# Two attention layers with expert layers on one core: tile counts, an even share of expert pieces in every pair, and the order of VectorE's work in it

## The chip, the core and the metric

The kernel runs on one core of a Trainium2 chip. The core has a matrix engine (TensorE, PE in the profile; PEld is its loading of weights), VectorE (DVE), ScalarE (ACT), GpSimd (POOL) and a sync engine (SP) that starts most transfers. Each engine runs its own list of instructions in order, and they meet by semaphores. The metric is the device time of one execution in microseconds (us), lower is better.

## The reference

The input is eight sequences of 512 rows, 256 wide. There are two layers, and each adds an attention and a mixture of experts to its input, both fed by the layer-normed rows:

```python
xn = _layernorm(x)
x = x + _L0_attn_ref(xn, ...) + _L0_ffn_ref(xn, ...)
xn = _layernorm(x)
x = x + _L1_attn_ref(xn, ...) + _L1_ffn_ref(xn, ...)
```

`_L0_attn_ref` is a latent attention (16 heads of 16) with a norm over each head of the queries and keys and a causal softmax. `_L0_ffn_ref` sends each row to 4 of 8 experts:

```python
gate = jnp.minimum(gate, SWIGLU_LIMIT)
up = jnp.clip(up, -SWIGLU_LIMIT, SWIGLU_LIMIT)
act = (up + 1.0) * gate * jax.nn.sigmoid(SWIGLU_ALPHA * gate)
```

`_L1_attn_ref` is a causal attention with sparsemax in place of softmax. `_L1_ffn_ref` has an own grouped-query attention with rotation, then 2 of 8 experts per row, whose activation is `silu(g) * u`, and a clipped residual.

## The kernel before

Each of the three attentions works on a sequence in eight **pairs** (two heads each): 3 attentions by 8 sequences by 8 pairs are 192 pairs, numbered G from 0. The first 64 pairs are the latent attention ("mla"), the next 64 the grouped one ("gqa"), the last 64 the sparse one ("spm"). In a sequence, p = G mod 8 numbers the pairs. The expert rows are sorted by expert beforehand into **tiles** of 256 rows, with each expert's rows padded to whole tiles. 4096 rows with 4 choices are 64 full tiles. Tiles beyond those in use hold padding and are computed all the same.

**Two stages carry experts beside attention.** `SPANS` gives them: pairs 0 to 49 carry the 72 tiles of the first layer, pairs 138 to 177 the 40 tiles of the second. A tile s is four halves of work with the inner width cut in two (m = 0, 1). In `plan` they are a list of **pieces**, for each m: "gate" (12 matmuls, L771, into bank2), "up" (12 matmuls, L771, into bank3) and "down" of the tile before (12 matmuls, L791, into bank4). The list is cut into equal shares for the pairs, and each share into six slots q = 0..5 that stand between the steps of the pair's attention. For 72 tiles in 50 pairs that is 432 pieces, 8 or 9 in a pair, and the cut falls on another piece in each pair. For 40 tiles in 40 pairs it is 6 in each.

**PE in a pair with experts** does: turn the shifted queries (L745, `bank<-ident,qst`), turn the output of the pair before (`bank<-ident,oT`), slot 0, first half of the key scores (L817, L827), turn queries and keys of the next pair (`ident,qst` and `ident,kst`), slot 1, second half of the key scores, slot 2, query scores of the next pair (L824), slot 3, their second half, slot 4, outputs (L894), slot 5, and in p = 1 to 4 a projection for the next sequence (L846, two banks). After each "up" with m = 0 it also turns the rows of the next tile (`bank<-ident,xs`).

**Banks.** In these stages the turns, projections and outputs share two banks, bank0 and bank1, in strict alternation (class `Ring`). A bank is free again when the engine that reads it says so. The turned rows of a tile are read twice: ScalarE rounds them into `xh` (L1422) and VectorE then makes the remainder `xl` (`rest`, L1637), which frees the bank.

**The activation of a half tile** in the first layer goes over four engines: VectorE clips the gate (`clip_gate`, L1649, frees bank2), ScalarE takes its tanh (`gate`, L1402), VectorE clips the up half (`clip_up`, L1663, frees bank3), then `multiply`: L1672 joins the tanh and L1675 makes the product `t`. ScalarE rounds it (`high`, L1417), GpSimd makes its remainder (`low`, L1240), and "down" may use both. `multiply` and, behind it, `rest` or `pick_weight` (L1629, L1632) are put off: they are done before the next "gate" or at three fixed places of the pair (`finish`). In the second layer ScalarE applies silu straight from bank2 and VectorE has the one product L1682.

**Other work of VectorE in a pair**: `heads_out` of the pair before (L1917 to L1923), in p = 0 the statistics of the next sequence (`row_stats`) and, at the end, its `normalize` (L1736), in p = 2 to 5 `head_squares`, then `maxima` (L1831 or L1829) and `shift` for the next pair. `norm_heads` (L1780 to L1788) scales queries and keys of the next mla sequence: four heads at the end of p = 5, twelve at the end of p = 6. GpSimd's `stack` for two pairs later waits for it at p = 0 and p = 2.

After the first stage GpSimd gathers expert outputs into the accumulator by indirect transfers (four pairs from the second after the stage, and from pair 55), and after the second one 16 units of such adds are shared by the pairs left.

Of the kernel before, what the change touches and what calls it, by code (L numbers as in the profile page):

```python
# [24 lines left out]
F32 = mybir.dt.float32  # L25
# [16 lines left out]
NTOK = B * T  # L42
TS = 256
# [6 lines left out]
CHOICES = (4, 2)  # L50
# [4 lines left out]
TILES = (72, 40)  # L55
FIRST_TILE = (0, 72)
SPANS = ((0, 50), (138, 178))
# [89 lines left out]
def build(nc, dram, outs, ctx):  # L147
# [494 lines left out]
    def pipeline(kinds, its, mems, em=None, general=False):  # L642
# [14 lines left out]
        for layer, (a, b) in enumerate(SPANS if em else ()):  # L657
# [66 lines left out]
        with block as block:  # L724

            @block.tensor
            def _(pe):
# [25 lines left out]
                def up(s, m, side):  # L753
# [10 lines left out]
                    if g >= 1:  # L764
                        pe.wait_ge(used, g)
# [467 lines left out]
            def _(pool):  # L1233
# [14 lines left out]
                def stack(G):  # L1248
# [10 lines left out]
                    if p == 2 and kind == "mla":  # L1259
# [133 lines left out]
            def _(act):  # L1393
# [225 lines left out]
            def _(dve):  # L1619
                chain = Chain(dve, dve_step)  # L1620
                late = []
# [31 lines left out]
                def clip_up(g):  # L1653
# [3 lines left out]
                    bias = em["gu"][s % 2][:, 2 * GU:2 * GU + 8].bitcast(F32)  # L1657
                    dve.wait_ge(u_full, g + 1)
                    if g >= 2:
                        dve.wait_ge(al_ready, g - 1)  # L1660
                    for h in range(2):
                        j = FC + 2 * m + h
                        ins = dve.tensor_scalar(t[:, TS * h:TS * (h + 1)], up_bank[:, TS * h:TS * (h + 1)],  # L1663
                                                bias[:, j:j + 1], LIMIT + 1.0, ALU.add, ALU.min)
                    ins.then_inc(u_used, 1)

                def multiply(g):

                    t = em["t"][g % 2]
                    if layer_of(g // 2) == 0:  # L1670
                        dve.wait_ge(th_ready, g + 1)
                        chain(dve.scalar_tensor_tensor(em["gc"][:, :], em["th"][:, :], 1.0, em["gc"][:, :],  # L1672
                                                       ALU.add, ALU.mult))
                        dve.wait_ge(u_used, g + 1)
# [10 lines left out]
                def experts(G, q):  # L1685
                    for what, s, i in plan[G][q]:
                        if what == "gate":
                            finish()
                            if layer_of(s) == 0:
                                clip_gate(2 * s + i)  # L1690
                        if what == "up":
                            if layer_of(s) == 0:
# [642 lines left out]
```

## Time and profile before

| | |
|---|---|
| time, three runs | 3400.03, 3402.33, 3407.31 us (median 3402.33) |
| the profiled execution | 3404.42 us, of which 3402.4 us are the traced span |
| PE, DVE, ACT, POOL busy | 85%, 64%, 49%, 42% of the span |
| mean granted PE clock | 0.968 |
| first stage with experts | about 320 to 1515 us |
| second stage with experts | about 2480 to 3231 us |

All pairs of the profile can be found by their 16 output matmuls (L894) on PE. The number in square brackets behind an instruction is the time for which its engine sat idle before it, and what ended that.

### The profile page before, as it was taken

The page shows a single profiled execution, that of the slowest core. Times are in us where ns is not written, and L with a number is a line of the kernel's source. Part 1 is how long each engine was busy: PE and PEld are TensorE (multiplying, and loading weights), DVE is VectorE, ACT ScalarE, POOL GpSimd, SP SyncE. Part 2 cuts the span into 40 slices and gives each one's busy share as a digit, 9 for nine tenths or more (in the row PEclk, how much of TensorE's full clock was granted, in tenths as well). Part 3 has the DMA queues.
Part 4 walks back from the last instruction along what each step waited for, and adds up shares of the span by engine and source line. Part 5 has one row for each costly group of instructions (what it writes and reads, how often), then busy time and mean ns, then how long its engine had stood idle before and what let it go on. Part 6 is the DMA issues. An engine that isn't in the chain of part 4 may idle for free. (4 is left out here: it accounts for less than half of the span.)

```text
span 3402.4 us, 61952 instructions
## 1 busy us (share of the span) xinstructions
PE 2902.5 (85%) x21678; PEld 2326.9 (68%) x21678; DVE 2166.4 (64%) x6249; ACT 1659.2 (49%) x3466; POOL 1433.8 (42%) x2037
## 2 busy tenths in 40 slices
PE   4414989989998999987998888898899999999996
PEld 3312778777878778775666666666578888888864
DVE  4544677777767677755777777766745455454565
ACT  1201445444454545444666665665545555555553
POOL 3753333424242433328555666532322222222277
PEclk9997999999999999988999999999899999999998
DMA  8852556556665666632233333322155555555455
GB/s 270 300 214 107 221 224 244 221 223 230 231 238 222 223 223 222 243 127 39 50 89 92 100 100 100 91 86 72 48 220 215 203 215 210 207 212 199 153 101 120
DMA packets 193735, 587.54 MB, mean 173 GB/s; under 512 B 22984, under 2 KB 145808, under 8 KB 158608
## 3 DMA queue, kind: packets, MB, share of 16 engines
q1 hardware_dynamic: 156560, 532.40, 42.5%
q0 software_dynamic: 36864, 51.14, 7.4%
q8 instruction: 177, 2.90, 0.3%
q14 instruction: 134, 1.10, 0.1%
HBM read 456.99 MB, written 126.48 MB: 171 GB/s over the span
## 5 line engine op out<-in xcount | busy, mean ns | idle before, releaser
L1240 POOL TENSOR_TENSOR al<-t,ah 128x512 fp32r<-128x512 f32 x224 | 293.2, 1309 | 1097.8 <-ACT ah L1417 1097.8
L771 PE MATMUL bank<-xh,gu 128*128 128x256 f32 x3584 | 658.8, 288 | 8.1 <-DVE t L1682 2.4
L817 PE MATMUL bank<-masks_bf,ident_bf 128*128 128x128 bf16 (+1 forms) x2304 | 579.1, 251 | 90.8 <-ACT ksT L1499 40.7
L1831 DVE TENSOR_REDUCE st<-bank 128x1 f32<-128x512 f32 (+3 forms) x1024 | 423.9, 482 | 208.1 <-PE bank L824 206.9
L1512 ACT ACTIVATE pt<-bank 128x512 f32<-128x512 f32 (+1 forms) x1152 | 513.4, 538 | 83.3 <-PE bank L827 81.0
L771 PEld LDWEIGHTS bank<-xh,gu 128*128 128x128 f32 x3584 | 523.2, 193 | 25.9 <-issue 17.2
L817 PEld LDWEIGHTS bank<-masks_bf,ident_bf 128*128 128x128 bf16 x2304 | 224.9, 98 | 358.2 <-issue 78.3
L827 PE MATMUL bank<-qaT,ksT 128*128 128x512 f32 (+3 forms) x1536 | 436.0, 391 | 0.0
L824 PE MATMUL bank<-ksT,qsT 128*128 128x512 f32 (+3 forms) x1536 | 434.7, 380 | 0.0
L1520 ACT ACTIVATE oT<-bank 128x512 f32<-128x512 f32 x192 | 114.4, 596 | 514.6 <-PE bank L894 514.6
L771 PE MATMUL bank<-xl,gu 128*128 128x256 f32 x1792 | 362.0, 284 | 0.0
L824 PEld LDWEIGHTS bank<-ksT,qsT 128*128 128x128 f32 x1536 | 282.9, 205 | 3.4 <-issue 1.3
L827 PEld LDWEIGHTS bank<-qaT,ksT 128*128 128x128 f32 x1536 | 280.7, 203 | 0.3
L771 PEld LDWEIGHTS bank<-xl,gu 128*128 128x128 f32 x1792 | 280.5, 193 | 0.0
L745 PE MATMUL bank<-ident,qst 128*128 128x128 f32 x1536 | 237.5, 278 | 49.1 <-POOL kst L1282 36.3
L791 PE MATMUL bank<-dn,ah 128*128 128x256 f32 x1792 | 263.5, 290 | 14.7 <-POOL al L1240 9.3
L1417 ACT ACTIVATE ah<-t 128x512 fp32r<-128x512 f32 x224 | 141.4, 631 | 252.6 <-DVE t L1675 213.8
L894 PE MATMUL bank<-pt,V 128*17 128x512 f32 (+3 forms) x3072 | 256.5, 453 | 0.7 <-ACT pt L1512 0.7
L1829 DVE MAX8 top<-bank 128x8 f32<-128x512 f32 (+3 forms) x512 | 213.7, 484 | 58.0 <-PE bank L824 55.5
L791 PEld LDWEIGHTS bank<-dn,ah 128*128 128x128 f32 x1792 | 231.8, 193 | 20.7 <-issue 20.7
L745 PEld LDWEIGHTS bank<-ident,qst 128*128 128x128 f32 x1536 | 178.3, 142 | 86.1 <-POOL kst L1282 39.4
L1319 POOL DMA_INDIRECT acc<-ys_scratch,slots x128 | 204.4, 1597 | 44.9 <-issue 34.2
(249 smaller groups left out, 5282.6 us busy)
## 6 DMA issues: line engine op xcount, KB each, us to landing
gu<-wu_scratch SPq DMA_DIRECT2D x112, 2056.0 KB, 7.8
dn<-wd_scratch SPq DMA_DIRECT2D x112, 1024.0 KB, 9.4
xs<-xs_scratch SPq DMA_DIRECT2D x112, 264.0 KB, 8.9
ys_scratch<-yb SPq DMA_DIRECT2D x112, 256.0 KB, 9.6
raw<-in_gu SPq DMA_DIRECT2D x16, 1024.0 KB, 10.6
wu_scratch<-hi SPq DMA_DIRECT2D x16, 1024.0 KB, 5.4
wu_scratch<-lo SPq DMA_DIRECT2D x16, 1024.0 KB, 4.0
xs_scratch<-empty SPq DMA_DIRECT2D x32, 264.0 KB, 3.2
```

What stands on the lines that cost most here:

```text
L745: mm = pe.transpose(bank[:, P * n:P * (n + 1)], b, ident[:, :])
L771: mm = pe.matmul(bank[:, TS * h:TS * (h + 1)], gu[:, col:col + P], x[s % 2][:, TS * k:TS * (k + 1)], start=(n == 0), stop=(n == len(terms) ...
L791: mm = pe.matmul(down_bank[:, D * half:D * (half + 1)], a[s % 2][:, j // 2, tok:tok + P], dn[:, part + D * j:part + D * (j + 1)], start=(n ...
L817: pe.matmul(bank[:, diag:diag + P * len(unit)], ident_bf[:, :], masks_bf[:, 0 if which == "q" else 1, 0:len(unit), :].rearrange("p n k -> ...
L824: mm = pe.matmul(bank[:, first:first + width], mem["qsT"][:, P * blk:P * (blk + 1)], ks[:, 0:width], start=False, stop=end, skip_group_che ...
L827: mm = pe.matmul(bank[:, first:first + width], ks[:, P * blk:P * (blk + 1)], mem["qaT"][:, T - width:T], start=False, stop=end, skip_group ...
L894: mm = pe.matmul(bank[q0:q0 + HD + 1, P * kb:T], V[n % 2][:, kb, vh, :], pt[:, j, PT_AT[kb]:PT_AT[kb] + T - P * kb], start=(kb < 2), stop= ...
L1240: pool.tensor_tensor(em["al"][s % 2][:, m, :], em["t"][g % 2][:, :], em["ah"][s % 2][:, m, :].bitcast(F32), ALU.subtract).then_inc(al_read ...
L1319: pool.indirect_dma_start(acc[:, NT * b + t, :], None, ys_dram, at, compute_op=ALU.add).then_inc(gathered[i], 16)
L1512: act.activation(to, frm, ACT.Relu if kind == "spm" else ACT.Exp).then_inc(s_act, 1)
L1829: ins = dve.max(top[:, 0, r, :], bank[:, first:first + width])
L1831: ins = dve.reduce_max(st[:, 0, r:r + 1], bank[:, first:first + width], AX.X)
```

## The change

The tile counts become 64 + 7 = 71 and 32 + 7 = 39, which is the most that the padding can need. The shares are fixed by `PIECES`: nine pieces in each pair of the first stage and six in each of the second, so the stages are pairs 0 to 47 (the last with three pieces) and 138 to 176. VectorE's `clip_up`, `multiply` and `finish` are joined in `activate`, which stands wholly at the "up" piece, in the order tanh product, clip of the up half, product. ScalarE's tanh and silu move from the "up" piece to the "gate" piece. `norm_heads` is cut 8 and 8, stands behind slot 0 of p = 6 and p = 7, and GpSimd waits for its second part at p = 4. `normalize` in p = 0 stands ahead of slot 2.

```diff
+TILES = tuple(NTOK * k // TS + E - 1 for k in CHOICES)
+FIRST_TILE = (0, TILES[0])
+PIECES = (9, 6)
+SPANS = tuple((a, a - -6 * t // n) for a, t, n in zip((0, 138), TILES, PIECES))
...
-                own = work[len(work) * (G - a) // (b - a):len(work) * (G - a + 1) // (b - a)]
+                own = work[PIECES[layer] * (G - a):PIECES[layer] * (G - a + 1)]
...
                     if g >= 1:
-                        pe.wait_ge(used, g)
+                        pe.wait_ge(used, 3 * g if used is u_used else g)
...
-                    if p == 2 and kind == "mla":
+                    if p == NP // 2 and kind == "mla":
...
                 def experts(G, q):
                     for what, s, i in plan[G][q]:
-                        if what == "up":
+                        if what == "gate":
                             highs()
                             gate(2 * s + i)
-                            late.append(2 * s + i)
+                        elif what == "up":
                             if i == 0 and not last_tile(s):
                                 take_x(s + 1)
-                        elif what == "down":
+                            late.append(2 * s + i)
+                        else:
...
+                def activate(g):
...
+                    if layer_of(s) == 0:
+                        bias = em["gu"][s % 2][:, 2 * GU:2 * GU + 8].bitcast(F32)
                         dve.wait_ge(th_ready, g + 1)
+                        dve.scalar_tensor_tensor(em["gc"][:, :], em["th"][:, :], 1.0, em["gc"][:, :],
+                                                 ALU.add, ALU.mult).then_inc(u_used, 1)
+                        dve.wait_ge(u_full, g + 1)
+                        if g >= 2:
+                            dve.wait_ge(al_ready, g - 1)
+                        for h in range(2):
+                            j = FC + 2 * m + h
+                            dve.tensor_scalar(t[:, TS * h:TS * (h + 1)], up_bank[:, TS * h:TS * (h + 1)],
+                                              bias[:, j:j + 1], LIMIT + 1.0, ALU.add, ALU.min).then_inc(u_used, 1)
+                        dve.wait_ge(u_used, 3 * (g + 1))
                         dve.scalar_tensor_tensor(t[:, :], t[:, :], 1.0 - LIMIT, em["gc"][:, :],
                                                  ALU.max, ALU.mult).then_inc(a_ready, 1)
...
                         if what == "up":
-                            if layer_of(s) == 0:
-                                clip_up(2 * s + i)
-                            late.append((s, i))
...
+                            activate(2 * s + i)
+                            if not last_tile(s):
+                                if i == 0:
+                                    rest(s + 1)
+                                else:
+                                    pick_weight(s + 1)
...
                     experts(G, 0)
+                    if is_at(n + 1, "mla") and p >= 6:
+                        norm_heads(n + 1, slice(H // 2 * (p - 6), H // 2 * (p - 5)))
                     experts(G, 1)
-                    finish()
...
+                    if n + 1 < nb and p == 0:
+                        normalize(n + 1)
                     experts(G, 2)
-                    finish()
```

On PE, the end of pair 2 of the first stage stood like this before. L771 into bank3 is an "up" piece with m = 0, L791 a "down" piece, L846 the projection:

```order
L771 MATMUL bank3<-xh0_1728,gu0_1732 128x256 x2
L745 MATMUL bank0<-ident,xs1_1727 128x128 x4
L791 MATMUL bank4<-dn1_1735,ah1_1715 128x256 x8
L791 MATMUL bank4<-dn1_1735,al1_1717 128x256 x4
L846 MATMUL bank1<-w_mla_1698,xT 128x512
L846 MATMUL bank0<-w_mla_1698,xT 128x512
L745 MATMUL bank1<-ident,qst1_1676 128x128 x4
L745 MATMUL bank0<-ident,oT_1685 128x128 x4
```

Now every pair from 1 to 46 holds down, gate and up, down, gate and up, down, gate and up in its slots. In pairs with odd p the last "up" has m = 0. This is the end of pair 1, line numbers one higher:

```order
L772 MATMUL bank3<-xh1_1729,gu1_1733 128x256 x2
L746 MATMUL bank0<-ident,xs0_1726 128x128 x4
L847 MATMUL bank1<-w_mla_1698,xT 128x512
L847 MATMUL bank0<-w_mla_1698,xT 128x512
L746 MATMUL bank1<-ident,qst0_1675 128x128 x4
L746 MATMUL bank0<-ident,oT_1685 128x128 x4
```

The turned tile rows (`xs`) and the second projection share bank0. The down piece that stood between them is gone from there.

On VectorE, the end of pair 14 (p = 6) and the start of pair 15 stood like this before; `both` is the first step of `heads_out`:

```order
L1649 TENSOR_SCALAR gc_1718<-bank2,gu1_1733 128x256 x2
L1663 TENSOR_SCALAR t1_1721<-bank3,gu1_1733 128x256 x2
L1672 SCALAR_TENSOR_TENSOR gc_1718<-th_1719,gc_1718 128x512
L1675 SCALAR_TENSOR_TENSOR t1_1721<-t1_1721,gc_1718 128x512
L1629 TENSOR_TENSOR wtmp_1725<-xs0_1726,gu0_1732 128x16
L1632 TENSOR_REDUCE wsel1_1723<-wtmp_1725 128x2
L1780 TENSOR_TENSOR qk_mla0_1692<-qk_mla0_1692,qkn_1699 128x4x192 x2
L1785 TENSOR_TENSOR qk_mla0_1692<-qk_mla0_1692,qkw_1700 128x4x192 x2
L1788 TENSOR_TENSOR qk_mla0_1692<-qk_mla0_1692 128x4x192
L1917 COPY both_1691<-bank1 128x136
```

Now the end of an odd pair of the first stage, behind its maxima, is two whole activations and the start of the next pair:

```order
L1650 TENSOR_SCALAR gc_1718<-bank2,gu0_1732 128x256 x2
L1661 SCALAR_TENSOR_TENSOR gc_1718<-th_1719,gc_1718 128x512
L1668 TENSOR_SCALAR t1_1721<-bank3,gu0_1732 128x256 x2
L1671 SCALAR_TENSOR_TENSOR t1_1721<-t1_1721,gc_1718 128x512
L1630 TENSOR_TENSOR wtmp_1725<-xs1_1727,gu1_1733 128x16
L1633 TENSOR_REDUCE wsel0_1722<-wtmp_1725 128x2
L1650 TENSOR_SCALAR gc_1718<-bank2,gu1_1733 128x256 x2
L1661 SCALAR_TENSOR_TENSOR gc_1718<-th_1719,gc_1718 128x512
L1668 TENSOR_SCALAR t0_1720<-bank3,gu1_1733 128x256 x2
L1671 SCALAR_TENSOR_TENSOR t0_1720<-t0_1720,gc_1718 128x512
L1638 TENSOR_TENSOR xl0_1730<-bank0,xh0_1728 128x512
L1903 COPY both_1691<-bank0 128x136
```

The instruction that joins the tanh (now L1661) has moved ahead of the clip of the up half (now L1668), and the head norm is no longer between the last activation and `both`.

## Rows read from the trace of the kernel before

**Rows 1.** The page, busy time of each engine (us, share of span, instructions)

```profile
PE 2902.5 (85%) x21678; PEld 2326.9 (68%) x21678; DVE 2166.4 (64%) x6249; ACT 1659.2 (49%) x3466; POOL 1433.8 (42%) x2037
```

**Rows 2.** Busy time by stretch; columns: stretch, us, PE, PEld, DVE, ACT, POOL, PEclk, DMA, GB/s

```profile
722.60:912.60 190.00, 176.35 (x1409) 153.07 (x1409) 139.56 (x334) 92.37 (x190) 70.03 (x85) 0.99 0.61 229
872.80:876.20 3.40, 2.97 (x14) 2.97 (x15) 0.83 (x4) 1.18 (x2) 1.69 (x6) 0.50 0.88 308
...
2493.50:3230.00 736.50, 710.41 (x5597) 601.44 (x5598) 367.12 (x1205) 383.29 (x781) 184.02 (x357) 1.00 0.55 202
```

**Rows 3.** Waits of PE from 320 to 1511: us in total, times, longest

```profile
PE bank L745 <- DVE xl L1637: 26.8, 17, 2.1
PE bank L745 <- DVE both L1918: 24.3, 9, 5.0
```

**Rows 4.** VectorE at the end of pair 23: start, us, instruction [idle before]

```profile
887.40 0.87 DVE L1649 TENSOR_SCALAR gc<-bank,gu 128x256 f32<-128x256 f32 x2
888.18 0.87 DVE L1663 TENSOR_SCALAR t<-bank,gu 128x256 f32<-128x256 f32 x2
888.97 0.69 DVE L1672 SCALAR_TENSOR_TENSOR gc<-th,gc 128x512 f32<-128x512 f32 x1
889.69 0.69 DVE L1675 SCALAR_TENSOR_TENSOR t<-t,gc 128x512 f32<-128x512 f32 x1
890.30 0.68 DVE L1637 TENSOR_TENSOR xl<-bank,xh 128x512 fp32r<-128x512 f32 x1
...
894.41 0.26 DVE L1918 TENSOR_TENSOR both<-both,bank 128x102 f32<-128x102 f32 x1
```

**Rows 5.** ScalarE in the same stretch

```profile
888.30 0.63 ACT L1402 ACTIVATE th<-gc 128x512 f32<-128x512 f32 x1 [7.02 <-DVE gc L1649]
...
890.42 0.63 ACT L1417 ACTIVATE ah<-t 128x512 fp32r<-128x512 f32 x1 [1.00 <-DVE t L1675]
...
891.80 0.63 ACT L1402 ACTIVATE th<-gc 128x512 f32<-128x512 f32 x1
```

**Rows 6.** PE from the outputs of pair 23 to those of pair 24

```profile
887.02 1.27 PE L894 MATMUL bank<-pt,V 128*17 128x512 f32 x16
...
892.04 0.63 PE L745 MATMUL bank<-ident,oT 128*128 128x128 f32 x4
...
895.38 0.60 PE L745 MATMUL bank<-ident,kst 128*128 128x128 f32 x4
...
908.29 1.27 PE L894 MATMUL bank<-pt,V 128*17 128x512 f32 x16
```

**Rows 7.** PE behind the last "up" of pair 47

```profile
1462.44 0.60 PE L745 MATMUL bank<-ident,qst 128*128 128x128 f32 x4
1465.15 0.63 PE L745 MATMUL bank<-ident,oT 128*128 128x128 f32 x4 [2.12 <-DVE xl L1637]
```

**Rows 8.** PE, projection at the end of pair 27

```profile
984.26 1.02 PE L846 MATMUL bank<-w_mla,xT 128*128 128x512 f32 x2
985.45 1.12 PE L846 MATMUL bank<-w_mla,xT 128*128 128x512 f32 x2 [0.16 <-DVE xl L1637]
```

**Rows 9.** PE behind pair 32 (two rows), and at the end of the first stage

```profile
1110.33 1.16 PE L745 MATMUL bank<-ident,xb 128*128 128x128 f32 x8 [2.85 <-DVE xb L1736]
1111.24 1.65 PE L791 MATMUL bank<-dn,ah 128*128 128x256 f32 x8
...
1512.29 2.04 PE L791 MATMUL bank<-dn,ah 128*128 128x256 f32 x8 [4.20 <-POOL al L1240]
```

**Rows 10.** VectorE, the twelve-head part of the norm behind pair 14

```profile
678.25 2.89 DVE L1780 TENSOR_TENSOR qk_mla<-qk_mla,qkn 128x768 f32<-128x768 f32 x2
...
683.03 0.96 DVE L1788 TENSOR_TENSOR qk_mla<-qk_mla 128x768 f32<-128x768 f32 x1
```

**Rows 11.** PE, pair 160 of the second stage, and pair 185 of the tail

```profile
2912.13 1.21 PE L745 MATMUL bank<-ident,xb 128*128 128x128 f32 x8 [0.57 <-DVE xb L1736]
...
3319.84 0.86 PE L745 MATMUL bank<-ident,qst 128*128 128x128 f32 x4 [2.39 <-POOL kst L1282]
```

More of the change, by code:

```diff
@@ L42 @@
 NTOK = B * T
+CHOICES = (4, 2)
 TS = 256
@@ L49 @@
 GB = 2 * GU + 16
-CHOICES = (4, 2)
 TABLE = 80
-TILES = (72, 40)
-FIRST_TILE = (0, 72)
-SPANS = ((0, 50), (138, 178))
+TILES = tuple(NTOK * k // TS + E - 1 for k in CHOICES)
+FIRST_TILE = (0, TILES[0])
+PIECES = (9, 6)
+SPANS = tuple((a, a - -6 * t // n) for a, t, n in zip((0, 138), TILES, PIECES))
 FIRST_GATHERS = 55
@@ L1620, in _ @@
                 chain = Chain(dve, dve_step)
-                late = []
                 def pick_weight(s):
@@ L1686, in experts @@
                     for what, s, i in plan[G][q]:
-                        if what == "gate":
-                            finish()
-                            if layer_of(s) == 0:
-                                clip_gate(2 * s + i)
+                        if what == "gate" and layer_of(s) == 0:
+                            clip_gate(2 * s + i)
                         if what == "up":
-                            if layer_of(s) == 0:
-                                clip_up(2 * s + i)
-                            late.append((s, i))
-                def finish():
-                    while late:
-                        s, i = late.pop(0)
-                        multiply(2 * s + i)
-                        if not last_tile(s):
-                            if i == 0:
-                                rest(s + 1)
-                            else:
-                                pick_weight(s + 1)
+                            activate(2 * s + i)
[4 more added lines that the diff above has]
+                                    pick_weight(s + 1)
                 def row_stats(n):
@@ L2041, in pair_with_experts @@
                         experts(G, q)
-                    finish()
                     if is_at(n - 1, "spm") and p == 1:
                         residual(n - 1)
-                    if n + 1 < nb and p == 0:
-                        normalize(n + 1)
-                    if is_at(n + 1, "mla"):
-                        if p == 5:
-                            norm_heads(n + 1, slice(0, 4))
-                        if p == 6:
-                            norm_heads(n + 1, slice(4, H))
                 def pair_alone(G):
@@ L2087, in pair_alone @@
                         normalize_again(n + 1)
-                    if is_at(n + 1, "mla"):
-                        if p == 5:
-                            norm_heads(n + 1, slice(0, 4))
-                        if p == 6:
-                            norm_heads(n + 1, slice(4, H))
+                    if is_at(n + 1, "mla") and p >= 6:
+                        norm_heads(n + 1, slice(H // 2 * (p - 6), H // 2 * (p - 5)))
                     if is_at(n, "gqa") and 1 <= p <= 3:
@@ L2107, in _ @@
                     chain(dve.tensor_scalar(mems["mla"]["qkw"][:, 0, :], mems["mla"]["qkw"][:, 0, :], 0.25, None, ALU.mult))
-                    norm_heads(0, slice(0, 4))
+                    norm_heads(0, slice(0, H // 2))
                 maxima(0, range(NU))
@@ L2111, in _ @@
                 if kinds[0] == "mla":
-                    norm_heads(0, slice(4, H))
+                    norm_heads(0, slice(H // 2, H))
                 for G in range(steps):
```

17 lines of the change are left out of this document (removed).

## The prediction

> **What bounds the kernel now.** The page first: PE is busy for 85% of the span and the next engine, VectorE, for 64% [rows 1]. So I read what PE does and waits for, stage by stage. In eight pairs of the first expert stage PE works 176.4 of 190.0 us at clock 0.99; in the second stage 710 of 736.5 us at 1.00 [rows 2]. The second is nearly full. The first has 13.6 us of idle PE in eight pairs, 1.7 per pair, and that is where the change can win or lose. The waits of PE there name VectorE at both ends: 26.8 us in 17 waits for `xl`, 24.3 us in 9 for `both` [rows 3]. Both free one of the two shared banks. VectorE is not the busiest engine but the one that is late at the end of a pair, because its maxima end late and two activations queue behind them [rows 4].
>
> **A pair that already stands in the new order.** From the outputs of pair 23 to those of pair 24 the pieces lie exactly as they will lie everywhere: gate and up, down, gate and up, down, gate and up, down. This takes 21.27 us (908.29 less 887.02 [rows 6]) with 9 pieces and no PE wait over 0.5 us. It is my yardstick. A pair of mean share takes 190.0 / 8 = 23.75 us for 8.64 pieces.
>
> **The change, part by part.**
>
> *Two tiles less.* A tile is six pieces of 12 matmuls, 1.44 us each by the spacing in the trace at full clock (one piece of 8 + 4 matmuls: 1.5 us at L791), and 0.44 us for turning its rows: 9.1 us. PE is the bound in both stages, so two tiles give -18.2 us. If one hid behind other waits it would be -9.
>
> *The end of the first stage.* Before, the last two downs wait 4.20 us for the last remainder from GpSimd [rows 9], then 0.66 us more, and 10 us pass at half clock, which costs some 5. Now two idle slots stand between the last up and the last downs. Two pairs also leave the stage and their 1.7 us of idle each. 4.9 + 5 + 3.4 is -13 us (bounds: 0, and -18 if all that PE idles in the last pairs goes).
>
> *Even shares, with VectorE's order as it was.* Eight yardstick pairs are 170.2 us. Four carry a projection, 2.2 us each (from 984.26 to 986.5 by both rows [rows 8]), 8.8; one carries the turned rows of the next sequence, 1.2 [rows 9]. In the four pairs behind an odd p the last up has m = 0, its turned rows hold a bank, and the second turn or projection behind it waits for `xl`: 2.12 us in pair 48 [rows 7], four times 8.4. Sum 188.6 us for 72 pieces. The stage before needs 190.0 for 69.1 pieces; 2.9 more at 1.44 make 194.1. So -5.5 us per eight pairs, and for 47 intervals -32 us. In this the wait for head norms (up to 5.0 us, once in eight pairs [rows 3]) is gone: the twelve-head part keeps VectorE from 678.25 to 683.99 ahead of `both` [rows 10]. Now two parts of eight heads, some 3.5 us each by the same rate, stand behind `both`, while PE does a down, three score units and two turns.
>
> *VectorE's new order in an activation.* This is the step that decides. Before, the clip of the up half (888.18, next start 888.97: 0.79 us) runs while ScalarE makes the tanh (888.30 to 888.93) [rows 4, 5]. The tanh costs VectorE nothing. Now L1672's step comes ahead of the clip. VectorE is idle from 888.2 to 888.97, then joins, clips and multiplies: `t` comes 0.79 us later. Two activations follow each other behind the maxima, both with VectorE late, so 1.6 us. ScalarE's `ah`, `yb` and `oT` now stand between the first product and the second tanh, by the spacing 890.42 to 891.80 [rows 5] another 0.3. `xl`, which frees the bank in the odd pairs, is 1.9 us later: 4 x 1.9 = 7.6 per eight pairs. In the even ones PE waits 0.75 us for bank3, since the up half is now clipped at 890.4 and not at 888.97 where PE wants it at 889.8 (1.44 behind the gate piece that starts at 888.3, when bank2 is free), and in two of them `both` (894.41 before) is late too, for a turn that PE wants at 895.4 [rows 4, 6]: 0.75 twice, 1.1 and 1.75, 4.3. Sum 11.9 us per eight pairs, +70 us for 47 intervals. Bounds: 0, if VectorE has slack there that I don't see, and +75 (two times 0.79 in each of 47 pairs).
>
> *The clock.* After a wait of 2.85 us the clock falls to half: a down takes from 1111.24 to 1113.5 us, 2.3 us, where it takes 1.5 at full clock [rows 9]; after 2.59 us it stands at 0.50 for 3.4 us [rows 2]. All nine such waits of PE of 2.59 us or more in this stage are followed by such a stretch, of some thirteen of about 2 us only two. The odd waits grow from 2.1 to about 3.2 us (the bank 1.9 later, PE itself 0.75 later), with a projection 2.8. A stretch loses half of 3.4 us, 1.7. Five of eight pairs could have one; I take three, +5.1 per eight pairs, +30 us (bounds 0 and +50). The Trainium skill ("TensorE: Matmul & The Clock Gate", HAM oscillation) describes the same for a loop in which each round waits: the penalty is paid in every round, as half of the throttled time. By that rule all five pairs pay and the sum is 20 us higher; the trace agrees on the half, and on two-microsecond waits it mostly doesn't pay.
>
> *Small parts.* `normalize` earlier in p = 0 ends a wait of 0.57 us in five pairs of the second stage [rows 11], -2.5. Tanh and silu move ahead on ScalarE: 0, its silu was already waiting for nothing but bank2, and the 1.07 us waits for `xl` in that stage stay, since `xh` waits for the turned rows. The 16 units of adds are now shared by 15 pairs and only the last has two: the 2.39 us wait [rows 11] goes, -2.4. The first norm at the start has 8 heads and not 4, +1.4. In pair 54, without experts, the norm now stands at VectorE's end and GpSimd's `stack` behind it, and the first thing PE does in pair 55 is to turn its result: about 3.5 for the norm, 2.3 for the stack, +6 (0 to +9). Bringing GpSimd's gathers two pairs forward: 0, they collide with the same kind of pair.
>
> **The sum** against the profiled execution, 3404.4: -18.2 - 13 - 32 + 70 + 30 - 2.5 - 2.4 + 1.4 + 6 = +39, so 3443.7. The median of the three runs is 2.1 us lower, and I predict 3441 us.
>
> **Rivals.**
>
> *A. VectorE's order costs nothing.* The even shares win and the new wait is absorbed, since VectorE is only 73% busy in this stage (139.6 of 190 [rows 2]). For it: the idle share. Against it: at the end of a pair VectorE works without a pause from 887.40 to 894.67 [rows 4], and a bank hangs on each end. Then 3404.4 - 18.2 - 13 - 32 + 2.5, about 3343 us. This is the other side, faster; it decides if the bank waits behind odd pairs stay near 2.1 us. From the sum it takes a cost of order plus clock under 55 us for any gain at all.
>
> *B. Order costs, clock doesn't.* The waits grow, but the clock stays up, as it did in most waits near 2 us. Then 3443.7 - 30 - 2.1, about 3411 us, and down to 3398 if the order also costs less than reckoned.
>
> *C. Every late bank is paid in full.* With a strict turn of two banks every delay of `xl` goes to PE at its full length, and all five waits in eight pairs take their stretch at half clock: 3441 plus two more stretches in eight pairs (1.7 x 2 x 5.9 = 20), 3461 us. For it: all nine waits of 2.59 us or more had one. Against it: with a projection the wait is 2.8 us only by my working. The Trainium skill ("Perfetto Trace Analysis", Optimization Strategy) reads the same gap repeating on the engine that should be full as a sign of too few buffers in PSUM; the 17 waits for `xl` [rows 3] agree.
>
> *D. It doesn't do what it says.* Tiles 72 and 40 might be in use. The bound of 71 follows from the padding, and a tile too few would change the result, not the time; I leave this no chance of its own.
>
> **How the numbers follow.** My forecast with its own range of 3420 to 3455 us: 0.45. C: 0.13. B: 0.17. A and what lies between it and no change: 0.25. Three runs of this kernel spread by 0.2%, so no change is within 6.8 us of 3402.3. Faster than 3395.5: A, 0.25, and a little of B, 0.02. Same: most of the lower half of B, 0.09. Slower: 0.64. The range of 8 in 10 leaves out the bottom of A and the top of C: 3348 to 3470 us. The likeliest case alone, slower, is 3410 to 3465.
>
> **What would show it.** Right: in pairs 1 to 46 the `oT` turn or the second projection behind odd p waits about 3 us for `xl`; PE waits some 0.7 us at bank3 ahead of the last up of a pair; VectorE shows an idle 0.7 us ahead of the tanh join, ended by ScalarE; eight pairs of the first stage take about 205 us, the clock there falls from 0.98 to about 0.95. Wrong on the order: eight pairs take 190 or less and the `xl` waits stay at 2. Wrong on the shares: waits in pairs with even p that the yardstick doesn't have. The second stage should keep its 151 us for eight pairs (736.5 / 39 x 8 [rows 2]) less 0.5, and the tail end 9 us after its tile. If GpSimd's `stack` shows up ahead of PE's turns at p = 7 within the stage, the head norms in two equal parts are what I mispriced.

## The result, and the profile after

The changed kernel takes 3424.86 us (median of 5 runs, 3419.56 to 3426.56), the kernel before 3400.03 us (5 runs of the same chip, 3388.92 to 3407.31). The ratio is 1.0066, with a 95% interval of 1.0046 to 1.0086: slower by 0.7%. The profiled executions are 3426.6 us (span 3424.9) and 3404.4 us (span 3402.4), so 22 us are to be explained; the forecast was +39.

First the busy line of the page after, against [rows 1]: two tiles less are 152 matmuls less, yet PE is busy only 2 us less.

```profile
PE 2900.2 (85%) x21526; PEld 2315.0 (68%) x21526; DVE 2171.0 (63%) x6229; ACT 1649.7 (48%) x3452; POOL 1435.1 (42%) x2033
```

Busy time by stretch (us, PE, PEld, DVE, ACT, POOL, PEclk, DMA, GB/s) from the outputs of pair 14 to those of pair 22, and from those of pair 0 to those of pair 47. In the kernel before the same eight pairs took 188.8 us. The 190.00 us of [rows 2] are another stretch (it starts 1.9 us behind the outputs of pair 16), but the mean of eight pairs over that stage is 190.0 too.

```profile
702.50:907.10 204.60, 184.45 (x1421) 158.62 (x1423) 142.81 (x337) 92.66 (x190) 72.01 (x85) 0.97 0.59 220
343.40:1534.00 1190.60, 1073.77 (x8253) 920.85 (x8252) 832.29 (x1951) 543.35 (x1115) 423.86 (x498) 0.97 0.59 217
```

What PE waits for in the first stage (343 to 1534 us; total, times, longest). The waits for `xl` are longer than in [rows 3], and a new group stands third: the bank of the up half, which L1668 reads.

```profile
PE bank L746 <- DVE xl L1638: 30.0, 11, 2.7
PE bank L847 <- DVE xl L1638: 26.1, 12, 2.2
PE bank L772 <- DVE t L1668: 22.2, 47, 0.5
PE bank L746 <- DVE both L1904: 11.6, 7, 1.8
PE bank L818 <- ACT pt L1514: 9.0, 6, 1.7
PE bank L746 <- ACT oT L1522: 4.9, 23, 0.3
```

Where it comes from is seen at the end of a pair. VectorE at the end of pair 23 (start, us, instruction, idle before), against [rows 4]:

```profile
930.94 0.87 DVE L1650 TENSOR_SCALAR gc<-bank,gu 128x256 f32<-128x256 f32 x2
932.51 0.69 DVE L1661 SCALAR_TENSOR_TENSOR gc<-th,gc 128x512 f32<-128x512 f32 x1 [0.70 <-ACT th L1403]
933.12 0.87 DVE L1668 TENSOR_SCALAR t<-bank,gu 128x256 f32<-128x256 f32 x2
934.02 0.69 DVE L1671 SCALAR_TENSOR_TENSOR t<-t,gc 128x512 f32<-128x512 f32 x1
...
936.78 0.69 DVE L1661 SCALAR_TENSOR_TENSOR gc<-th,gc 128x512 f32<-128x512 f32 x1 [0.99 <-ACT th L1403]
937.38 0.87 DVE L1668 TENSOR_SCALAR t<-bank,gu 128x256 f32<-128x256 f32 x2
938.29 0.69 DVE L1671 SCALAR_TENSOR_TENSOR t<-t,gc 128x512 f32<-128x512 f32 x1
938.90 0.68 DVE L1638 TENSOR_TENSOR xl<-bank,xh 128x512 fp32r<-128x512 f32 x1
```

And PE in the same place: it waits for the clip of the up half, then for `xl`.

```profile
934.04 0.51 PE L772 MATMUL bank<-xh,gu 128*128 128x256 f32 x2 [0.43 <-DVE t L1668]
936.37 0.63 PE L746 MATMUL bank<-ident,qst 128*128 128x128 f32 x4 [0.19 <-ACT oT L1522]
939.73 0.63 PE L746 MATMUL bank<-ident,oT 128*128 128x128 f32 x4 [2.73 <-DVE xl L1638]
```

That is VectorE's idle time ahead of the join, ended by ScalarE. It stands there in nearly every activation; its sum from 368 us to the end of the stage, where the kernel before has less than 1 us of it:

```profile
DVE gc L1661 <- ACT th L1403: 102.4, 137, 1.1
```

Along the program, by the start of a pair's outputs on PE (L895, before L894), the changed kernel is 43.2 us behind at pair 56 (1659.4 against 1616.2), 43.4 at pair 137, 28.2 at pair 178 and 22.5 at the end of the span. So the first stage and the pairs behind it lose 43 us, and the second stage with the tail wins 21.

### The profile page after: what moved, and what is told of

It is laid out like the page before. It is cut to its first block and busy times, and to the rows that moved or that the text cites. A ratio compares the mean times of both kernels' runs of the same rounds, so it can differ in the third digit from the quotient of the medians.

```text
span 3424.9 us, 61408 instructions
## 1 busy us (share of the span) xinstructions
PE 2900.2 (85%) x21526; PEld 2315.0 (68%) x21526; DVE 2171.0 (63%) x6229; ACT 1649.7 (48%) x3452; POOL 1435.1 (42%) x2033
## 5 line engine op out<-in xcount | busy, mean ns | idle before, releaser
L1241 POOL TENSOR_TENSOR al<-t,ah 128x512 fp32r<-128x512 f32 x220 | 286.3, 1301 | 1131.0 <-ACT ah L1418 1131.0
L772 PE MATMUL bank<-xh,gu 128*128 128x256 f32 x3520 | 636.8, 287 | 31.5 <-DVE t L1668 22.2
L772 PEld LDWEIGHTS bank<-xh,gu 128*128 128x128 f32 x3520 | 502.7, 190 | 62.7 <-DVE t L1668 31.6
L772 PE MATMUL bank<-xl,gu 128*128 128x256 f32 x1760 | 351.8, 281 | 0.0
L772 PEld LDWEIGHTS bank<-xl,gu 128*128 128x128 f32 x1760 | 271.4, 190 | 0.0
L1403 ACT ACTIVATE th<-gc 128x512 f32<-128x512 f32 x142 | 89.6, 631 | 370.7 <-DVE gc L1650 370.7
L895 PE MATMUL bank<-pt,V 128*17 128x512 f32 (+3 forms) x3072 | 256.3, 453 | 0.7 <-ACT pt L1514 0.7
L1418 ACT ACTIVATE ah<-t 128x512 fp32r<-128x512 f32 x220 | 138.6, 630 | 205.5 <-DVE t L1671 144.5
```

The costliest lines, as they stand in the source:

```text
L772: mm = pe.matmul(bank[:, TS * h:TS * (h + 1)], gu[:, col:col + P], x[s % 2][:, TS * k:TS * (k + 1)], start=(n == 0), stop=(n == len(terms) ...
L895: mm = pe.matmul(bank[q0:q0 + HD + 1, P * kb:T], V[n % 2][:, kb, vh, :], pt[:, j, PT_AT[kb]:PT_AT[kb] + T - P * kb], start=(kb < 2), stop= ...
L1241: pool.tensor_tensor(em["al"][s % 2][:, m, :], em["t"][g % 2][:, :], em["ah"][s % 2][:, m, :].bitcast(F32), ALU.subtract).then_inc(al_read ...
L1418: act.activation(em["ah"][s % 2][:, m, :], em["t"][g % 2][:, :], ACT.Copy).then_inc(ah_ready, 1)
```

## The experiments

Each differs from its base by the edit shown alone. "Stage" is the time from the outputs of pair 0 to those of pair 47 (before: to pair 49, 1163.9 us), "passage" from there to those of pair 57 (before: 118.3 us; changed: 1190.6 and 134.0). The kernel before was run again beside experiments 1 to 4, 5 to 8 and 9 to 12, with medians of 3403.9, 3399.3 and 3403.6 us. So kernels of different groups are compared by their ratios to it, and not by their medians.

**1. The clip first again** (base: the changed kernel; the counts of `u_used` that PE and VectorE wait for follow the edit).

```diff
 def activate(g):
+    # u_full, al_ready; clip both halves -> u_used
     dve.wait_ge(th_ready, g + 1)
     # join: gc <- (th + 1) * gc
-    # u_full, al_ready; clip both halves -> u_used
     # product: t -> a_ready
```

> The changed kernel with one thing put back: in an activation of the first expert layer VectorE clips the up half first and joins the tanh after it. Tiles, shares, norms and tail stay as changed. My theory (the order costs, the even shares win): `xl` comes 1.9 us earlier, the waits of PE for it behind odd pairs fall from 2.7 to about 2.1 us and the one ahead of the last up of a pair (0.5 us) goes; the 47 intervals of the stage fall from 1190.6 to about 1110 to 1125 us and the kernel takes 3345 to 3360 us. Rival 1 (the order costs nothing, the shares themselves are dear): within 5 us of the changed kernel, 3420 to 3430. Rival 2 (half and half): 3380 to 3395, with `xl` waits still above 2.4 us.

Measured: 3347.49 us, ratio to the kernel before 0.983 [0.9816, 0.9843]; stage 1110.3 us. PE's waits and the stage's busy time:

```profile
PE bank L746 <- DVE xl L1638: 21.4, 11, 2.0
PE bank L847 <- DVE xl L1638: 16.6, 12, 1.4
PE bank L746 <- ACT V L1475: 7.4, 24, 0.4
```

```profile
345.10:1455.40 1110.30, 1040.47 (x8257) 901.92 (x8259) 829.32 (x1951) 540.77 (x1115) 423.83 (x498) 0.99 0.63 233
```

One order of two VectorE steps is worth 77 us by the medians and 80 by the ratios. The group at L772 is gone, the waits for `xl` are 0.8 us shorter each. The stage's difference of 80.3 us is 47.0 us of idle PE (116.8 against 69.8) and 33.3 us of busy PE for the same matmuls. Part of the busy time is the clock (71.7 us at half clock against 27.3). Another part is found in the gate and up matmuls alone, of which none ran at half clock in either kernel (the stage again, PE and PEld of L772, first the changed kernel, then this one):

```profile
343.40:1534.00 1190.60, 437.20 (x3336) 406.53 (x3336) 0.97 0.59 217
345.10:1455.40 1110.30, 424.88 (x3336) 403.64 (x3336) 0.99 0.63 233
```

The same 3336 matmuls keep PE busy for 12.3 us more. The 47 waits at bank3 are the difference: a matmul that starts behind a pause adds 0.38 us of busy time here, and one in the stream 0.12.

**2. The join first, in the kernel before.**

```diff
 # multiply(g), at the next gate piece or at the pair's end
     join: gc <- (th + 1) * gc
+    clip_up(g)
     product: t
 # experts(): "up"
-    clip_up(2 * s + i)
```

> The kernel before with one thing changed: VectorE joins the tanh first and clips the up half behind it, in every activation of the first expert layer. Tiles, shares and all else as before. Theory: the order costs by itself, with the old uneven shares as well; 0.8 us per activation, where a bank hangs on it, so +40 to +70 us, 3440 to 3470. Rival 1 (the order is harmless until the shares are even): within 7 us of the kernel before. Rival 2 (the old shares leave slack in most pairs): +10 to +30 us.

Measured: 3453.34 us, ratio 1.0147 [1.0132, 1.0161], so +50 us. The order costs by itself, also with the old shares; of PE's waits in its stage (`both`, 21.7 us in 9, is near [rows 3]):

```profile
PE bank L745 <- DVE xl L1637: 34.3, 21, 2.9
PE bank L771 <- DVE t L1663: 13.7, 20, 0.8
PE bank L745 <- ACT V L1473: 11.7, 24, 1.6
```

**3. Two tiles less, in the kernel before.**

```diff
-TILES = (72, 40)
-FIRST_TILE = (0, 72)
+TILES = (71, 39)
+FIRST_TILE = (0, 71)
```

> The kernel before with 71 and 39 tiles, all else as it was (the pieces are still spread over 50 and 40 pairs). Theory: PE bounds both stages, 9.1 us per tile, -18 us, 3382. Rival 1: one of the two hides behind waits of the first stage, -9 us, 3391. Rival 2: a tile less only lengthens the waits for the shared banks, within 5 us of the kernel before.

Measured: 3402.11 us, ratio 0.9994 [0.9984, 1.0005]. The second rival: no gain that can be measured. The profile shows 10.7 us won up to the outputs of pair 56 and given back in the second stage, which takes 770.9 us from pair 138 to 178 and took 760.6 with a tile more. 234 pieces in 40 pairs are 5.85 a pair; the pieces wander through the slots, and new waits come up (here 2482 to 3253 us):

```profile
PE bank L745 <- DVE xb L1736: 5.7, 5, 2.1
PE bank L745 <- ACT oT L1520: 5.5, 6, 1.6
PE bank L854 <- DVE xl L1637: 5.2, 4, 1.5
```

**4. Even shares alone, in the kernel before** (the stage ends after 48 pairs).

```diff
+PIECES = (9, 6)
-SPANS = ((0, 50), (138, 178))
+SPANS = tuple((a, a - -6 * t // n) for a, t, n in zip((0, 138), TILES, PIECES))
-own = work[len(work) * (G - a) // (b - a):len(work) * (G - a + 1) // (b - a)]
+own = work[PIECES[layer] * (G - a):PIECES[layer] * (G - a + 1)]
```

> The kernel before with nine and six pieces in each pair, so that the first stage ends after 48 pairs and not 50; 72 and 40 tiles, VectorE's order, the head norms and the tail's adds as before (but GpSimd's gathers move two pairs forward with the end of the stage). Theory: even shares give 45 us in the stage and at its end, and the pairs without experts behind it take some 12 us of that back, as in the changed kernel's trace (109.4 against 125.4 us to the outputs of pair 56): 3360 to 3372 us. Rival 1: the even shares win nothing, since every pair with odd p now stalls: 3395 to 3405. Rival 2: they lose: over 3410.

Measured: 3426.26 us, ratio 1.0066 [1.0052, 1.008]: slower, and my theory for this kernel fell (rival 2). Its stage takes 1163.7 us, 53.4 more than the first experiment's: 31.5 us of idle PE, and 78.5 us at half clock against 27.3. Two waits hold most of the idle time, for the head norms ahead of `both` and for `normalize`:

```profile
PE bank L746 <- DVE both L1919: 29.2, 6, 4.9
PE bank L746 <- DVE xl L1638: 21.4, 11, 1.9
PE bank L746 <- DVE xb L1737: 17.1, 6, 2.9
```

So what I had booked as the gain of even shares belongs to the shares together with two moves of VectorE's other work. Experiments 7 and 8 take these apart.

**5. Head norms a pair earlier behind the stage** (base: experiment 1).

```diff
 # pair_alone
-if is_at(n + 1, "mla") and p >= 6:
-    norm_heads(n + 1, slice(H // 2 * (p - 6), H // 2 * (p - 5)))
+if is_at(n + 1, "mla") and 5 <= p <= 6:
+    norm_heads(n + 1, slice(H // 2 * (p - 5), H // 2 * (p - 4)))
```

> The first experiment's kernel (clip first; 3347.5 us), with the two halves of the head norm at the ends of pairs 53 and 54 instead of 54 and 55, in pairs without experts alone. Theory: in pair 54 GpSimd's `stack` waits 11.1 us for the norm there, and PE then 6.8 us for `kst`; that PE wait falls to 2 or 3 us, and the kernel takes 3341 to 3344 us. Rival 1: GpSimd is late on its own account (four powers of some 5.5 us, two stacks and the gathers in these pairs), the wait is merely renamed, within 2 us of 3347.5. Rival 2: VectorE does the norm ahead of the maxima that PE's next scores wait for in pair 53, and loses elsewhere: 3348 to 3352.

Measured: 3339.94 us, ratio 0.9825 [0.9811, 0.9839]; the ratios don't tell it from experiment 1. The passage takes 130.5 us and not 134.6: 4.1 us by the profile. The stage ahead of it, in which nothing differs, was 4.0 us shorter than in experiment 1, so half of the difference of the profiled executions (8.5 us) is not the edit's.

**6. Gathers in pairs 51 to 54 again** (base: experiment 1).

```diff
-if em and ends_at[0] < G <= ends_at[0] + CHOICES[0]:
+if em and ends_at[0] + 2 < G <= ends_at[0] + 2 + CHOICES[0]:
     for i in range(2):
-        gather(0, G - ends_at[0] - 1, i)
+        gather(0, G - ends_at[0] - 3, i)
```

> The first experiment's kernel (3347.5 us), with the gathers of the first rows in pairs 51 to 54, where the kernel before has them, and no longer in 49 to 52. Theory: a gather's four issues cost GpSimd some 8 us in a pair that already has a power and a stack; the waits of PE for `kst` in pairs 50 to 52 (2.7, 3.9 and 6.0 us) shrink by 3 to 6 us in all, of which the later pairs, with the norm, give back some: 3340 to 3345. Rival: pairs 53 and 54 then carry both, the loss only moves, 3347 to 3353.

Measured: 3339.90 us, ratio 0.9824 [0.981, 0.9837], again not told from experiment 1 by the ratios; passage 128.5 us, 6.1 less. The step that I had priced at nothing is seen on GpSimd in the changed kernel, ahead of the pair whose `kst` comes 5.89 us late: a power, four gathers, and only then the stack.

```profile
1593.18 5.45 POOL L1307 TENSOR_TENSOR qkn<-qkn,minus_half 128x32 f32<-128x32 f32 x1
1598.82 1.62 POOL L1320 DMA_INDIRECT acc<-ys_scratch,slots  x1 [0.19 <-issue]
...
1604.97 1.54 POOL L1320 DMA_INDIRECT acc<-ys_scratch,slots  x1 [0.81 <-issue]
1605.94 0.88 POOL L1273 CAST qst<-qk_mla 128x128 fp32r<-128x128 f32 x1
...
1608.34 0.29 POOL L1283 COPY kst<-kst 128x128 f32<-128x128 f32 x1
...
1624.99 0.29 POOL L1273 CAST qst<-qk_mla 128x128 fp32r<-128x128 f32 x1 [10.95 <-DVE qk_mla L1774]
```

The last row is the wait for the head norm that the prediction named, in pair 54. PE's part, on the turns of the stacks of these pairs:

```profile
1593.27 0.85 PE L746 MATMUL bank<-ident,qst 128*128 128x128 f32 x4 [4.58 <-POOL kst L1283]
1608.68 1.11 PE L746 MATMUL bank<-ident,qst 128*128 128x128 f32 x4 [5.89 <-POOL kst L1283]
1627.16 1.12 PE L746 MATMUL bank<-ident,qst 128*128 128x128 f32 x4 [6.81 <-POOL kst L1283]
```

**7. Head norms as before** (base: experiment 1).

```diff
 # pair_with_experts, pair_alone, at their ends
-norm_heads in halves at p = 6, 7
+if p == 5: norm_heads(n + 1, slice(0, 4))
+if p == 6: norm_heads(n + 1, slice(4, H))
 # GpSimd's second wait for them: p == NP // 2 -> p == 2
```

> The first experiment's kernel (3347.5 us), with the head norms as in the kernel before: four heads at the end of p = 5, twelve at the end of p = 6. Theory: the wait of PE for `both` in the stage goes from 6 back to about 29 us, as in the kernel with even shares alone, and takes some half-clock stretches with it: 3375 to 3390 us. Rival 1: with VectorE's activations in one go the long part finds room, 3350 to 3360. Rival 2: at the stage's end it wins back what the pairs 53 to 55 lose, the whole 3365 to 3375.

Measured: 3366.76 us, ratio 0.9904 [0.9888, 0.9919], to experiment 1 +19 us by the profiled executions and +25 by the ratios: the second rival's size. The stage loses 27.5 us (1137.8), `both` is back, and the passage wins 6.6 (128.0). The row is from 368 us on; the whole stage has 36.1 us in 12 waits.

```profile
PE bank L746 <- DVE both L1905: 29.6, 10, 4.9
```

**8. `normalize` as before** (base: experiment 1).

```diff
 # pair_with_experts
-    if n + 1 < nb and p == 0:      # ahead of the third slot
-        normalize(n + 1)
 ...
+    if n + 1 < nb and p == 0:      # at the end
+        normalize(n + 1)
```

> The first experiment's kernel (3347.5 us), with `normalize` back at the end of pairs with p = 0. Theory: PE's wait for `xb` comes back, 2.9 us in each of five or six such pairs of the first stage (14 to 17 us in the kernel with even shares alone) and with some of them a stretch at half clock, 1.7 us; in the second stage 0.5 us in five pairs: 3363 to 3375 us. Rival: the turn of the rows moves behind other PE work that is there anyway, 3348 to 3355.

Measured: 3351.77 us, ratio 0.986 [0.9845, 0.9876], +10 us to experiment 1 by the ratios and by the profiled executions; stage 1115.8 us, +5.5. The wait of the theory is there (the row is from 368 us on; in the whole stage six waits, 17.1 us), but the price is nearer the rival's: those for `both` at the same turn (6.2 us) go, so that idle PE grows by 8.4 us.

```profile
PE bank L746 <- DVE xb L1723: 14.2, 5, 2.8
```

**9. Both moves of 5 and 6** (base: experiment 1; the two edits above together).

> The first experiment's kernel (clip first) with both moves at the end of the first stage: the halves of the head norm in pairs 53 and 54, the gathers in pairs 51 to 54. Theory: the two relieve different engines, and what each gave from the outputs of pair 47 to those of pair 57 (134.6 us, 130.5 with the norm moved, 128.5 with the gathers moved) adds up: about 124.5 us, 3330 to 3336 us in all. Rival: both relieve the same pile-up on GpSimd, 128 us, 3338 to 3342.

Measured: 3340.54 us, ratio 0.9812 [0.9799, 0.9825]; passage 122.8 us, 11.8 less than in experiment 1, so in the profile the two add up, and the passage of experiment 11, which has the same code there, takes 122.7. The times don't show it: the median lies in the rival's range (3338 to 3342), and the ratios don't tell 5, 6 and 9 apart.

**10. `xl` ahead of the product** (base: experiment 9).

```diff
 # activate, first layer: clip, join,
+    if between is not None:      # m = 0: the next tile
+        rest(between)            # xl
     dve.wait_ge(u_used, g + 1)
     # product: t -> a_ready
```

> The kernel of the ninth experiment with one more step: in the first expert layer VectorE makes `xl` of the next tile ahead of the product of the activation and not behind it. Theory: PE's waits for `xl` behind odd pairs (23 of them, 2.0 and 1.4 us) fall by 0.7 us each, 16 us in all, and a few stretches at half clock with them: 3312 to 3322. Rival: `t`, then `ah` and `al` come 0.7 us later and the downs or the next gate wait instead, within 4 us of the ninth. Rival 2: `xh` isn't there yet when VectorE asks for it and all of the activation waits: slower than the ninth by over 5 us.

Measured: 3325.94 us (3319.96 to 3327.17), ratio 0.9769 [0.9756, 0.9782], the fastest of all: 2.3% under the kernel before, 2.9% under the changed one. It missed the expected range all the same (3312 to 3322). The waits for `xl` fell by 14 us of the 16 reckoned; `oT` took part of it (9.6 us in 14 waits). The profiled execution is 15.5 us shorter than that of experiment 9: 7.9 us in the stage, 2.3 in the passage and 5.7 in pairs 57 to 137, where the edit changes nothing. So about half of the difference is placed at the edit. In the stage PE is busy 1032.1 of 1098.2 us at clock 1.00:

```profile
PE bank L746 <- DVE xl L1638: 14.8, 11, 1.4
PE bank L746 <- ACT oT L1522: 9.6, 14, 0.9
PE bank L847 <- DVE xl L1638: 9.4, 12, 0.8
```

```profile
343.60:1441.80 1098.20, 1032.08 (x8257) 890.61 (x8259) 845.05 (x1950) 540.02 (x1115) 422.73 (x498) 1.00 0.63 235
```

**11. The tail's adds in 14 pairs** (base: experiment 9).

```diff
-tail_pairs = range(ends_at[1], steps)
+tail_pairs = range(ends_at[1] + 1, steps)
```

> The kernel of the ninth experiment with the tail's 16 units of adds shared by the last 14 pairs and not by 15, as in the kernel before (two of them carry two). It prices the tail's part of the change. Theory of the prediction: +2.4 us. What the two traces say (28.2 us behind at the outputs of pair 179, 20.7 at the end): +7 us, with a stretch or two at half clock behind the wait for `kst`. Rival: nothing, since the last adds end the kernel in either case: within 2 us.

Measured: 3343.70 us, ratio 0.9823 [0.981, 0.9836]. From the outputs of pair 179 to the end it takes 140.0 us and the ninth kernel 134.1: 5.9 us. By the medians alone (+3.2, intervals overlap) it would be open, but all five profiled kernels with 14 pairs take 138.6 to 140.0 us there, and all nine with 15 take 132.6 to 134.1. PE shows a wait for `kst`, as in [rows 11], and one for the maxima behind it:

```profile
3264.35 0.66 PE L746 MATMUL bank<-ident,qst 128*128 128x128 f32 x4 [2.08 <-POOL kst L1283]
...
3279.43 0.28 PE L818 MATMUL bank<-masks_bf,ident_bf 128*128 128x256 bf16 x1 [1.74 <-DVE top L1816]
```

**12. The changed kernel with `xl` ahead of the product** (the edit of 10 in the changed kernel's order: join, clip, `xl`, product).

> The changed kernel as it is (tanh joined first, norms and gathers as changed), with `xl` of the next tile made ahead of the product. It asks how much of the order's cost hangs on the late `xl` and on the clock behind it. Theory: the 23 waits for `xl` (2.7 and 2.2 us) become 2.0 and 1.5, which is 16 us, and most of the 13 additional stretches at half clock go, up to 22 us: 3387 to 3409; the waits of PE at bank3 (47 of 0.5 us) stay. Rival 1: the clock's stretches don't depend on the length of these waits and stay at some 21: 3405 to 3412. Rival 2: PE then waits for `t` or `al`: within 7 us of 3424.9.

Measured: 3408.37 us (12 runs), ratio 1.0014 [1.0005, 1.0023], 16 us under the changed kernel, between theory and first rival. The waits at bank3 stayed, those for `xl` fell, and the clock rose from 0.97 to 0.99. The stage's 20.3 us are 13.7 us of busy PE and only 6.6 of idle (`oT` and `V` give back 10 us of the 17 that `xl` wins):

```profile
343.60:1513.90 1170.30, 1060.06 (x8257) 906.42 (x8260) 840.54 (x1951) 542.15 (x1115) 420.02 (x498) 0.99 0.60 221
```

```profile
PE bank L772 <- DVE t L1668: 22.2, 47, 0.5
PE bank L746 <- DVE xl L1638: 22.0, 11, 2.0
PE bank L847 <- DVE xl L1638: 17.3, 12, 1.5
```

## Why the prediction came out as it did

The direction and the mechanism were right and the size was 16 us too large. That it came so near is in part luck, since the smaller terms missed both ways (the gathers cost 6 us where I had 0, the tail won 5.9 where I had 2.4). Eight pairs took 204.6 us, where the sign said about 205, and the clock there was 0.97, not 0.95. Two readings of the prediction were loose: of the waits near 2 us in the stage before there are ten and not thirteen (two of them with a stretch at half clock), and 190 us is the mean of eight pairs, not a stretch from outputs to outputs. Step by step:

*Even shares with VectorE's order as it was*: forecast 188.6 us for eight pairs, 1108 for 47 intervals. Five profiled kernels have just this stage (experiments 1, 5, 6, 9, 11): 1110.3, 1106.3, 1106.4, 1106.1 and 1112.6. Right, but the gain hangs on the moves beside them: even shares alone lose (experiment 4). Of the 53 us between that stage and this one the norms in halves hold 27.5 (experiment 7) and the earlier `normalize` 5.5 (experiment 8). The rest, some 20, is the clock. Idle PE adds up (24.7 and 8.4 us against 31.5), but the stage of experiment 4 has 78.5 us at half clock, experiment 1 has 27.3, experiment 7 44.4 and experiment 8 23.9. That is 37.5 us more than the two moves bring one by one, and half of it is 19 us. Of its 12 stretches 11 last 6.8 us and not 3.4. Why they do, and what the activation in one go has to do with it, is not shown.

*VectorE's order, +70, and the clock, +30*: together 100, measured 80 in the stage and 77 in the medians (experiment 1). This is the term that was mis-sized. Between the two profiles the waits for `xl` grow by 18 us, those at bank3 by 22, `both` by 5, `pt` and `oT` by 7, less 4 for `V`; idle PE by 47 us in all. I had 45 for the late `xl` (PE's own delay with it) and 25 for the even pairs. `xl` comes 1.6 us later (7.96 against 6.38 us behind the start of the first `clip_gate`), where I had 1.9. PE arrives 0.8 us later by itself, for bank3 and `oT`, and the waits grow by 0.8 us, where I had 1.1. The bank3 wait is 0.5 and not 0.75 us, in every pair. But the restart behind it, which I had at nothing, keeps PE busy for 12.3 us more in 47 pairs (experiment 1), 0.26 us each. So the delay of a pair at bank3 is 0.73 us, 34.5 in all, and the 0.75 of the forecast (in the odd pairs as PE's own delay) was right in sum and wrong in its parts. The turn behind `both` I put at 17 us, of which 8 were more than bank3's delay, and it cost 5.

*The clock, part of it*: I expected some 17 stretches at half clock from the longer waits. There are 21, but with the old order 8 stand there too, so the order adds 13, 22 us by my 1.7 us each. A wait of PE in the changed kernel, the rows behind it, and the clock there:

```profile
838.20 1.12 PE L847 MATMUL bank<-w_mla,xT 128*128 128x512 f32 x2 [2.17 <-DVE xl L1638]
840.91 1.99 PE L792 MATMUL bank<-dn,ah 128*128 128x256 f32 x8
```

```profile
839.20:842.60 3.40, 3.37 (x17) 3.00 (x16) 1.20 (x4) 1.77 (x4) 1.24 (x1) 0.51 0.94 389
```

The clock stands at its lower level (1.2 GHz, 0.51 granted) right behind the wait, and eight matmuls take 1.99 us and elsewhere 1.11. So waits of 2.2 us mostly pay, where I had said that those near 2 us mostly don't. The remaining 11 us by which PE is busier than in experiment 1 are the restarts behind bank3. Rival B (order costs, clock doesn't) falls with this, rival A with experiments 1 and 2. Rival C, all waits paid in full, is nearer on the clock (18 of the 23 waits for `xl` have a stretch) and falls on the waits, which grew by less than I forecast. The Trainium skill ("TensorE: Matmul & The Clock Gate", HAM oscillation) describes a loop with longer waits, for transfers, and there each round pays. Here it is 18 of 23 rounds at 2.2 and 2.7 us, and in experiment 1 none of 12 at 1.4.

*Two tiles, -18.2*: not as a term of its own. Alone they give 2 us that can't be told from none (experiment 3). In the changed kernel the second stage, from pair 138 to 178, takes 747.7 us for 760.6: -12.9, where -9.1 for the tile and -2.5 for `normalize` were forecast. In these runs a tile less pays where a pair leaves the stage with it.

*The end of the first stage, -13, and pair 54, +6; the gathers, 0*: the 4.20 us wait is gone as forecast, but the passage carries 11.8 us that two small moves take away (experiment 9), where I had 6. The -13 for the end itself was not measured alone. The norm cost 4; the missed step is "bringing GpSimd's gathers forward: 0, they collide with the same kind of pair", which cost 6. I had read which kind of pair they meet and not how much GpSimd already does in it: a power of 5.45 us, four gathers of 1.9 each and a stack of 2.1, 15.5 us from 1593.18 to 1608.63; pair 48, which has none of it, takes 10.2 us.

*The tail, -2.4*: 5.9 (experiment 11). I took only the wait for `kst` in [rows 11]; behind it came a second wait and, in experiment 11, 3.4 us at half clock from 3280.4 us on.

*The start, +1.4*: the outputs of pair 0 stand at 343.4 us for 342.9, +0.5. *The second stage's waits for `xl`*, said to stay: 1.1 us, 17 times. Yes.

In sum: what is not order or clock was forecast at -61 and measured, by experiment 1, at -56; order and clock at +100 and +77 (+80 by the two ratios). In the traces the 80 are 34.5 for bank3 with its restarts (forecast 0.75 in 47 pairs, 35), 18 for the longer waits for `xl` (1.9 less 0.75 in 23.5 pairs, 27), 5 for `both` (8), 3 for other turns (0) and some 20 to 22 for the clock (30). So what was mis-sized is `xl`, whose waits grew by 0.8 and not 1.1 us, and the clock.

## What to carry to other kernels

Where two engines hand over a shared buffer in a fixed turn, look at an engine's idle time of a few tenths of a microsecond inside a step that holds the buffer: work that has its data (the clip) belongs ahead of work that waits (the join), and the release of the buffer (`xl`) ahead of what nobody waits for yet. One such order was worth more than all the balancing around it (80 us against 56). A short wait costs more than it shows: here each 0.5 us of idle PE at bank3 brought 0.26 us of restart with it. Balance of pieces by itself lost 22 us here: price it with all else that shares the engine at that place, and a removed piece of work only with the pair, or the wait, that goes with it. Where work moves to other steps, add up what the helper engine already does there.

## What the runs showed of the hardware

The waits of PE from 0.9 us up in the stage, counted over PE's rows, and how many were followed within 3.6 us by a stretch of 3.4 us at half clock:

| kernel | near 1.0 | near 1.4 | 1.5 to 1.8 | near 2.0 | 2.2 | 2.7 |
|---|---|---|---|---|---|---|
| changed | 0 of 1 | - | 3 of 11 | - | 10 of 12 | 8 of 11 |
| experiment 12 | 0 of 1 | 0 of 11 | 2 of 12 | 8 of 11 | - | - |
| experiment 1 | 0 of 12 | 0 of 12 | - | 8 of 11 | - | - |
| experiment 5 | 3 of 12 | 0 of 12 | - | 3 of 11 | - | - |
| experiment 6 | 3 of 12 | 0 of 12 | - | 3 of 11 | - | - |
| experiment 9 | 3 of 12 | 0 of 12 | - | 3 of 11 | - | - |
| experiment 11 | 0 of 12 | 0 of 12 | - | 10 of 11 | - | - |
| experiment 10 | 1 of 12 | 0 of 11 | - | - | - | - |

The first stage's code is the same in experiments 1, 5, 6, 9 and 11, and waits near 2.0 us paid 8, 3, 3, 3 and 10 times: 1110.3, 1106.3, 1106.4, 1106.1 and 1112.6 us. Pairs 57 to 137, whose work no edit touches, took 845.0 to 851.7 us in the ten profiles of kernels built from the changed one. The three shortest had 44 to 55 us at half clock there, the others 61 to 75. Much of the spread between runs of one kernel, some 0.2%, may be this; one profile of each doesn't show it. It also means that a few microseconds between two profiled executions are an edit's only where they stand at the edit.

A GpSimd cast of `qst` is recorded with 0.88 us behind the issue of gathers and with 0.29 elsewhere (1605.94 and 1624.99 above). It isn't slower: its row starts while the last gather's still runs (1604.97 to 1606.51) and ends 0.31 us behind it. So such rows can't be added up.
